# Column terms added by GpSimd instead of TensorE, row terms after the second norm, a rebuilt order, and 24 unused matmuls at the start

## The reference, cut to what matters

```
xn  = layernorm(x)                                   # x: 2 batches x 1024 tokens x 2048
q   = lambda v, s, z: (clip(round(v/s + z), 0, 255) - z) * s
x   = x + q(xn, s1, z1) @ q(ctx, s2, z2)            # ctx: 2 x 2048 x 2048
y   = layernorm(x)
x   = x + y @ W + bias + lora(y)                     # W: 2048 x 2048, LoRA rank 32 + 32 shared, 8 gates
```

## Time and profile before

| | |
|---|---|
| median of 3 runs | 1066.53 us |
| the profiled execution: its time | 1063.74 us |
| its span on the core | 1061.7 us |
| TensorE busy | 1003.1 us (94%) |
| VectorE, ScalarE, GpSimd busy | 532.3, 311.5, 163.4 us |
| mean granted TensorE clock | 0.989 of full speed |

### The profile page before, as it was taken

The page is one execution under the profiler, slowest core; times in us unless marked ns, Lnnn a source line. Parts: engine busy times, 40 slices in busy tenths (PEclk is TensorE's granted clock), DMA queues, the critical chain, the costliest instruction groups (busy, mean ns, idle before and its releaser), DMA issues.

```text
span 1061.7 us, 12294 instructions
## 1 busy us (share of the span) xinstructions
PE 1003.1 (94%) x4791; PEld 472.9 (45%) x4791; DVE 532.3 (50%) x764; ACT 311.5 (29%) x266; POOL 163.4 (15%) x199
## 2 busy tenths in 40 slices
PE   2778999799999999999999999999999999999996
PEld 1345444355544444444444444445544444444442
DVE  6754677879655455463423555987632023014010
ACT  4666731322032132232223743532121021003000
POOL 3101100101102211311510000020104004004110
PEclk9989999899999999999999999999999999999998
DMA  8869682767735446338599844456935025004010
GB/s 365 255 192 368 260 346 96 184 139 183 201 127 195 168 149 212 138 112 251 204 299 262 336 179 159 80 166 147 222 110 169 20 80 187 20 30 158 10 42 27
DMA packets 124392, 181.70 MB, mean 171 GB/s; under 512 B 96064, under 2 KB 96064, under 8 KB 111808
## 3 DMA queue, kind: packets, MB, share of 16 engines
q1 hardware_dynamic: 109600, 118.25, 37.3%
q0 software_dynamic: 13600, 58.73, 15.3%
q10 hardware_dynamic: 1152, 4.19, 1.0%
HBM read 128.72 MB, written 29.36 MB: 149 GB/s over the span
## 4 chain that ended last, share of the span: by engine, by line
PE 68%; DVE 11%; DMA 10%; issue 4%; ACT 3%; POOL 1%; SPq 1%; DVEq 0%; POOLq 0%; ACTq 0%
PE psum L1154 16%; PE psum L1156 16%; PE psum L1155 16%; PE psum L987 15%; DMA stage<-in_w 2%; DMA x<-in_x 2%; PE psum L1177 2%; DMA lhs<-in_lora_b 1%; DVE ring L1396 1%; DMA xn<-in_x 1%; DVE stats L1421 1%; DVE hl L1441 1%; DVE stats L1308 1%; DMA bias_sb<-in_bias 1%; DMA lhs<-ap_st 1%
## 5 line engine op out<-in xcount | busy, mean ns | idle before, releaser
L1154 PE MATMUL psum<-ring,lhs 128*128 128x512 f16 x1024 | 388.8, 380 | 9.4 <-DMA lhs<-hl 7.4
L1155 PE MATMUL psum<-ring,lhs 128*128 128x512 f16 x1024 | 388.8, 380 | 0.0
L1156 PE MATMUL psum<-ring,lhs 128*128 128x512 f16 x1024 | 388.8, 380 | 0.0
L987 PE MATMUL psum<-ring,lhs 128*128 128x512 bf16 x1024 | 235.2, 386 | 9.0 <-DMA lhs<-ap_st 7.1
L987 PEld LDWEIGHTS psum<-ring,lhs 128*128 128x128 bf16 x1024 | 101.4, 99 | 134.8 <-issue 15.4
L1154 PEld LDWEIGHTS psum<-ring,lhs 128*128 128x128 f16 x1024 | 100.3, 98 | 132.3 <-issue 10.1
L1156 PEld LDWEIGHTS psum<-ring,lhs 128*128 128x128 f16 x1024 | 100.4, 98 | 121.3 <-issue 0.8
L1155 PEld LDWEIGHTS psum<-ring,lhs 128*128 128x128 f16 x1024 | 100.3, 98 | 119.9 <-issue 0.8
L1448 DVE SCALAR_TENSOR_TENSOR x<-psum,sc,x 128x512 f32<-128x512 f32 (+1 forms) x64 | 45.3, 746 | 182.2 <-PE psum L1166 181.4
L748 ACT ACTIVATE ring<-stage,sc 128x2048 f16<-128x2048 f32 x32 | 63.7, 2002 | 202.6 <-PE psum L1156 159.4
L617 POOL TENSOR_TENSOR x<-x,bias_sb 128x512 f32<-128x512 f32 (+1 forms) x64 | 87.7, 1396 | 173.5 <-DVE xn L1431 98.2
(11 more groups left out here) (158 smaller groups left out, 644.9 us busy)
## 6 DMA issues: line engine op xcount, KB each, us to landing
stage<-in_w SPq DMA_DIRECT2D x38, 1024.0 KB, 6.0
stage<-in_ctx_in SPq DMA_DIRECT2D x30, 1024.0 KB, 7.9
out<-x POOLq DMA_DIRECT2D x64, 256.0 KB, 3.5
x<-in_x POOLq DMA_DIRECT2D x8, 1024.0 KB, 11.9
xn<-in_x POOLq DMA_DIRECT2D x8, 1024.0 KB, 7.3
x<-in_x POOLq DMA_DIRECT2D x4, 2048.0 KB, 15.9
lhs<-in_lora_a POOLq DMA_DIRECT2D x4, 1024.0 KB, 6.9
lhs<-in_lora_b SPq DMA_DIRECT2D x4, 1024.0 KB, 13.3
```

The costliest lines, as they stand in the source:

```text
L987: last = pe.matmul(psum[:, t, :], lhs_q[:, k, t * P:(t + 1) * P], ring_q[:, g, j % 2, u, :], start=(k == 0), stop=False)
L1154: pe.matmul(psum[:, t, :], hi, ring[:, g, 0, u, :], start=(kk == 0), stop=False)
L1155: pe.matmul(psum[:, t, :], hi, ring[:, g, 1, u, :], start=False, stop=False)
L1156: last = pe.matmul(psum[:, t, :], lo, ring[:, g, 0, u, :], start=False, stop=False)
```

## The change

1. Blocks other than block 0 of batch 0 lose the matmuls of L1021 (`column_term`, 8 a block, 7 blocks) and VectorE's `column_low`. ScalarE writes the whole column term to `bias_sb` in float32 (`col_row`), and GpSimd adds it to `x2` before the eviction (`add_column`, 8 a block); `evict1` waits for `with_col`.
2. The row term is added after `norm2` of a tile, 2048 columns at once, since a number per token does not change a layer norm; `add_bias` of block 0 waits for it.
3. Other orders: the loads, transposes and statistics of the opening, the LoRA loads and copies, VectorE's stream at the hand-over, and `base0_pair`, which starts on tile 0 alone.
4. Ahead of the first `turn`, TensorE does 24 matmuls of 512 columns into bank 0 whose result nobody reads.

The diff, cut to its core:

```
@@ sync
-            load_ctx(0, 1, [0, 1])
             for t in range(PT, TILES):
                 turn_q(t)
+            load_ctx(0, 1, [0, 1])
...
             load_lora_b(0)
+            load_lora_b(1)
             load_ctx(0, 1, [2])
-            load_lora_b(1)
-            load_ctx(0, 1, [3])
             load_lora_b(2)
             load_lora_b(3)
+            load_ctx(0, 1, [3])
+            sp.wait_ge(be_full, 8)
             load_ctx(0, 2, [0, 1])
...
-                        turn_y(b, 1)
+                        turn_high(b, 1)
+                    if g == 2 and isinstance(j, int) and j == 0:
+                        turn_low(b, 1)
@@ gpsimd
-            load_x([4, 5])
+            load_x(range(4, TILES))
             root_pair(1)
-            load_x([6, 7])
...
+            load_lora_a(0)
+            load_lora_a(1)
             root_pair(2)
-            load_lora_a(0)
             root_pair(3)
-            load_lora_a(1)
...
+            def add_column(b, j, tiles=range(TILES)):
+                pool.wait_ge(col_row, b * NBLK + j)
+                if b:
+                    pool.wait_ge(res_in[j], 16)
+                for t in tiles:
+                    if b == 0:
+                        pool.wait_ge(relued, t + 1)
+                    v = x2[:, t, j * NW:(j + 1) * NW]
+                    pool.tensor_tensor(v, v, bias_sb[:, :], ALU.add).then_inc(with_col, 1)
...
-                        pool.wait_ge(normed2, b * TILES + t + 1)
+                        pool.wait_ge(with_row, b * TILES + t + 1)
...
                     largest(1, MX_A, PW_A)
+                    add_column(b, 1, range(2))
                     largest(2, MX_B, PW_B)
-                    store_a(b)
-                    largest(3, MX_W, PW_W)
+                    add_column(b, 1, range(2, TILES))
                 else:
                     load_residual(b, NBLK - 1)
-                    store_a(b)
+                    add_column(b, 0)
+                    add_column(b, 1)
+                store_a(b, [0, 1])
+                add_column(b, 2)
+                store_a(b, [2, 3])
+                add_column(b, 3, [0])
+                if b == 0:
+                    largest(3, MX_W, PW_W)
+                add_column(b, 3, range(1, TILES))
@@ scalar, column(j)
-                    act.activation(col_parts[:, n % 2, :], psum[:, CB, :], ACT.Copy, scale=D1).then_inc(col_hi, 1)
+                    if n == 0:
+                        act.activation(col_parts, psum[:, CB, :], ACT.Copy, scale=D1).then_inc(col_hi, 1)
+                    else:
+                        if n > 1:
+                            act.wait_ge(with_col, (n - 1) * TILES)
+                        act.activation(bias_sb[:, :], psum[:, CB, :], ACT.Copy, scale=D1F).then_inc(col_row, 1)
+
+                def row_term(t):
+                    act.wait_ge(rows_ready, b + 1)
+                    act.activation(x2[:, t, :], x2[:, t, :], ACT.Identity, bias=RC[:, t:t + 1]).then_inc(with_row, 1)
@@ scalar, batch 0 after the row sums
-                    act.wait_ge(rows_ready, b + 1)
-                    for t in range(TILES):
-                        row_term(t, 0, 1)
                     for c in range(NBLK):
                         for k in range(c * KC, (c + 1) * KC):
                             a_eff_out(k)
-                        ctx_block(b, 1, [c])
+                        if c < 2:
+                            ctx_block(b, 1, [c])
+                    ctx_block(b, 1, [2])
                     for c in range(NBLK):
+                        if c == NBLK - 1:
+                            ctx_block(b, 1, [3])
                         b_eff_out(c)
-                        if c:
-                            row_term(c - 1, 1, NBLK)
@@ scalar, second norm
                     split_hi(b, t)
                     if t + 1 < TILES:
                         root(b, 1, t + 1)
+                    row_term(t)
...
                 split_hi(b, 1)
+                w_groups(b, 0, [2, 3])
                 root(b, 1, 2)
-                w_groups(b, 0, [2, 3])
+                row_term(0)
+                row_term(1)
@@ tensor
+                pe.wait_ge(ident_ready, 1)
+                pe.wait_ge(pats, 6)
+                for n in range(24):
+                    pe.matmul(psum[:, 0, :], ones_b, any_row, start=True, stop=True)
                 turn(0)
                 turn(1)
...
+                if t == CB and (b or j):
+                    pe.wait_ge(col_row, b * NBLK + j)
...
-                    for t in range(2):
-                        tile_in(t)
-                        bank_free(k, t)
-                    for g in range(NG):
+                    tile_in(0)
+                    bank_free(k, 0)
+                    pe.wait_ge(converted, grp_w(b, 0, 0) + 1)
+                    base_group(0, 0)
+                    high_in(1)
+                    bank_free(k, 1)
+                    high_group(1, 0)
+                    pe.wait_ge(converted, grp_w(b, 0, 1) + 1)
+                    base_group(0, 1)
+                    low_in(1)
+                    low_group(1, 0)
+                    base_group(1, 1)
+                    for g in range(2, NG):
@@ vector, evict1
-                dve.wait_ge(with_row, (2 + j) * TILES + t + 1 if b else min(j, 1) * TILES + t + 1)
+                if b or j:
+                    dve.wait_ge(with_col, (b * NBLK + j - 1) * TILES + t + 1)
@@ vector, opening
             stats1(4)
             round1(2)
+            round1(3)
             stats1(5, range(2))
-            round1(3)
...
+            scale_rows([4, 5], 3)
             head_group(3)
-            stats1(6)
-            scale_rows([4, 5], 3)
+            stats1(6, range(2))
+            round1(4)
+            stats1(6, range(2, NBLK))
+            round1(5)
             stats1(7)
             variance([6, 7])
-            round1(4)
             scale_rows([6, 7], 4)
-            round1(5)
@@ vector, hand-over
                 evict1(b, j, 3)
-                early_stats2(b, 2)
-                late_stats2(b, 2)
+                w_group(b, 0, 0)
                 low2(b, 1)
                 evict1(b, j, 4)
                 evict1(b, j, 5)
-                w_group(b, 0, 0)
                 w_group(b, 0, 1)
                 evict1(b, j, 6)
                 evict1(b, j, 7)
                 w_group(b, 0, 2)
+                stats2(b, 2)
                 w_group(b, 0, 3)
```

More of the change, by code:

```diff
@@ L1120, in first_by_tile @@
                         column_sum(b, j)
-                    first = 1 if tail else TILES // 2 - 1
-                    if t >= first:
-                        column_term(b, j, range(t + 1) if t == first else [t])
                 if tail:
@@ L1129, in first_by_tile @@
                             group1(j, t, g)
-                    column_term(b, j, range(TILES - tail, TILES))
             def base(b, t, j, k, gi):
@@ L1146, in last_bases, with high_group, low_group @@
                         base_group(t, g)
+            def high_group(t, g):
+                for u in range(GU):
+                    kk = g * GU + u
+                    hi = lhs[:, 0, kk, t * P:(t + 1) * P]
+                    pe.matmul(psum[:, t, :], hi, ring[:, g, 0, u, :], start=(kk == 0), stop=False)
+                    pe.matmul(psum[:, t, :], hi, ring[:, g, 1, u, :], start=False, stop=False)
+            def low_group(t, g):
+                for u in range(GU):
+                    lo = lhs[:, 1, g * GU + u, t * P:(t + 1) * P]
+                    pe.matmul(psum[:, t, :], lo, ring[:, g, 0, u, :], start=False, stop=False)
             def base_group(t, g):
```

97 lines of the change are left out of this document (49 added, 48 removed).

## The result

| | before | after |
|---|---|---|
| median | 1066.41 us (4 runs, 1064.5 to 1067.35) | 1082.03 us (4 runs, 1078.03 to 1082.87) |
| ratio, 95% interval | | 1.0141 [1.0117, 1.0165] |
| profiled execution's span | 1061.7 us | 1076.5 us |

What follows compares the result with a forecast made beforehand. TensorE, busy 1003.1 of 1061.7 us, was taken as the bound. Terms -8.6 - 4.6 - 4.8 - 4.5 - 5.2 - 2.3 + 4.5 = -25.5, +0.5 for the clock, gave -25: median about 1041 us, range 1033 to 1055.

Steps and rivals of the forecast that it cites:

- column matmuls: First product: 56 of 64 matmuls go, 12.1 us of PE time; GpSimd's 56 adds instead cost PE nothing.
- Opening and LoRA: Start of batch 0: earlier transposes give -8.6 us, LoRA B waits removed -4.6; block 1 starts at 96.2.
- row terms: ScalarE: 48 instructions become 16 of 2048 columns, each hidden while VectorE does low2; costed at nothing.
- Fewer matmuls: First product: 0.216 us saved per column matmul; -4.8 us in batch 0's blocks 1 and 2, -5.2 in batch 1.
- Hand-over: Start of second product: PE starts without pause and VectorE's chain gains; -4.5 us in batch 0, -2.3 in batch 1.
- Contention: GpSimd and VectorE on shared SBUF ports, moved add_bias meeting norm2 and hand-over meetings: +4.5 us, bounds 0 and 9.
- Rival C: GpSimd's adds pace the blocks, from 3.45 us an add; at 4.2 us the time is 1081 us; chance 0.03.
- 24 unused matmuls: Ahead of the first turn: up to 0.7 us late or 0.8 faster, hidden both ways; 0.
- -7.5 predicted for batch 1: Batch 1: -5.2 us from fewer matmuls in blocks 0 to 2 and -2.3 from VectorE's hand-over chain.

Runs made afterwards that it cites:

- e1: The changed kernel with GpSimd's first three all-reduces replaced by an elementwise operation: 1052.42 us, ratio 0.9866.
- e8: e4 with the hand-over to the second product of the kernel before, in both batches: 1051.41 us, ratio 0.9878.
- e10: The changed kernel with VectorE's context groups 2 and 3 ahead of the evictions of block 1 in batch 0: 1074.59 us, ratio 1.0071.
- e6: The kernel before with only the new order of loads, transposes and VectorE's statistics in the opening, LoRA loads included: 1062.34 us, ratio 0.9971.
- e4: The changed kernel with batch 0's column terms by matmul as before and batch 1's by GpSimd: 1051.59 us, ratio 0.9877.
- e5: e4 with the column terms of batch 1 by matmul too, so no GpSimd column adds anywhere: 1057.36 us, ratio 0.9926.
- e11: The changed kernel with all 56 adds, largest(1) and largest(2) together, largest(3) behind block 3's adds, context groups first, no unused matmuls: 1055.75 us, ratio 0.9915.
- e12: e11 with the column sum of blocks 1 and 2 behind tile 2 instead of tile 0, both batches: 1053.15 us, ratio 0.9893.
- e3: The changed kernel without the 24 unused matmuls: 1079.07 us, ratio 1.0149.
- e9: The kernel before with only the row terms moved behind norm2 of each tile: 1066.31 us, ratio 1.0006.
- e7: The kernel before with one 128x1 GpSimd add between all-reduces largest(1) and largest(2) in batch 0: 1067.01 us, ratio 0.9998.
- e2: The changed kernel with largest(1) and largest(2) together and all eight adds of block 1 behind them: 1071.73 us, ratio 1.0057.

## Why the prediction was wrong

The sign was wrong because of one step, and two terms were too large. The step is worth the 29.6 us between after and e1. The rest, 11 us from my 1041 to e1's 1052.42, is for the larger part the hand-over, 6.8 us in the sum and 0 in e8.

*The step that failed* is in "column matmuls": that `add_column(0,1)` "stands behind four stores and the first all-reduce, with `largest(2)` in its middle; the evictions behind it are needed only a block later", and that `largest(3)` and the seven last adds "come before" the evictions that need them. I counted instructions (1.27 us an add, 0.4 an all-reduce) and not what lies between two kinds of them. The trace of before had it: its first all-reduce began at 120.34, with GpSimd idle for 6.3 us before it, put down to "issue", after its last store, and its first add at 209.02 had 8.4 us of the same ahead of it. In its place the runs show 34.5 us of change-over on the chain of after, 29.6 us of time from after to e1. The second half of the sentence was wrong as well: evictions held by the adds hold the context groups behind them on VectorE (after) and bank 7 for the column sum (e10).

*Opening and LoRA* were right to a microsecond: the LoRA matrices at 67.0 (67.7), block 1 at 96.6 (96.2), the transpose wait gone. But the term alone is not worth 13 us: e6, with the orders of that term and not the others, gave 3.4. The row terms I had costed at nothing, and the order of the copies I had not costed at all; one of them, or both, let the 13 us arrive.

*Fewer matmuls* pay where nothing disturbs the adds: 5.8 of 6.9 us in batch 1 (e4 against e5). In batch 0 the term (-4.8) is there once no change-over stands among the adds: from the column sum of block 1 to that of block 3 e1 takes 55.7 us, e4 59.1 and the kernel before 60.6. In the whole time it is not seen: e1, e11 and e12 are no quicker than e4.

*Hand-over, -4.5 and -2.3:* wrong in size. In e4 the fourth group's load came late, behind a transpose, which I had left out of the step "load of W's fourth group (about 5.4 here)": it was issued 32.1 us after block 3's column sum and landed at 38.1. So `norm2(2)` gained 0.8 us (44.1 to 43.4) where I had 4.5, and the row terms took some 1.6 back. In after itself it came 45.6 us behind that column sum, 1.5 later than before. TensorE's pause at `delta0(2)`, predicted at some 4 us, was 2.83 in after and 3.18 in e4. e8 prices the whole term at 0, within some 5 us.

*Contention, +4.5:* present, but not where I had put it. Beside the moved `add_bias` three `norm2` of batch 0 took 1.48 us instead of 1.35, 0.13 each where I had 0.4. The larger part came from the column adds, which I had not counted here. In batch 1 of after one context group met a series of eight adds, as both timelines show:

```profile
603.96 9.85 POOL L618 TENSOR_TENSOR x<-x,bias_sb 128x512 f32<-128x512 f32 x8
...
609.67 4.70 DVE L1421 TENSOR_SCALAR ring<-ring 128x2048 bf16<-128x2048 int16 x1
```

The groups over the whole run, by line, count, busy time, mean and idle time, against the earlier trace rows:

```profile
L618 POOL TENSOR_TENSOR x<-x,bias_sb 128x512 f32<-128x512 f32 x56 | 83.3, 1519 | 64.2 <-ACT bias_sb L917 40.6 <-issue 23.5
...
L1421 DVE TENSOR_SCALAR ring<-ring 128x2048 bf16<-128x2048 int16 x30 | 27.9, 932 | 51.6 <-ACT ring L768 51.5
```

That context group took 4.70 us instead of 0.69 and ended 0.6 us after the last add: it was held over more than three adds, not for one. The evictions beside the same series stayed at 0.75. The Trainium skill (SBUF — State Buffer, Who interferes with whom) has both: a VectorE `tensor_scalar` in a mode that takes the shared ports is fully blocked by a GpSimd instruction that holds them, and an instruction with one SBUF input outside such a mode is not touched; that a series of adds can keep the ports from one to the next is this trace's. Over all 30 groups it is 7.2 us of VectorE (27.9 - 20.7). In e4, with adds in batch 1 alone, it is 5.7 us (26.4 - 20.7), of which the time shows 1 to 2 (6.9 less 5.8 or 5.2), less than the spread of the runs.

*Rival C* named GpSimd and 1081 us, and the time came out there, but not by its mechanism: it decided from 3.45 us an add, and the adds took 1.52. I had given it 0.03, having looked for the price of the adds and not of what stands between them. My argument that much of VectorE's 19.31 us in a block is evictions was also loose: eight of 0.746 us are 6.0.

*The 24 unused matmuls* at 0, and *row terms* at nothing, held (e3, e9).

**Left open.** The stretch of loops between the batches took 303.0 us before and 303.6 to 307.3 in the other kernels; TensorE's pauses there sum to 3.1 us before, 5.7 in after and 7.2 in e12. Batch 1 took 471.0 us before, 469.7 in after, and from 465.6 (e3) to 475.5 (e10) in kernels whose batch 1 is the same as that of after. These are single profiles, and no experiment addressed the differences. So the -7.5 predicted for batch 1 is neither shown nor refuted by the two profiles; what is shown is e4 against e5.

## What to carry to other kernels

GpSimd's stream is priced by its changes of kind, not only by its instructions: look for idle time put down to "issue" ahead of an all-reduce or behind one, and keep elementwise work that someone waits for away from it, or let the all-reduces stand together. When an instruction is made later, find every reader of the bank or buffer that it frees, the odd one first: here the column sum uses bank 7 one tile after the block's start. And a reordering that "costs nothing" may be what another part's gain rests on; the opening alone was worth 3.4 us, though block 1 started 12 us earlier.

## What the runs showed of the hardware

- GpSimd's change-over: 5.6 to 5.8 us from adds to an all-reduce and 6.9 to 9.5 from there to adds in after; around the 0.47 us add of e7 it was the other way round, 10.39 to the all-reduce and 6.75 from it. Two all-reduces together take one change-over (10.05 us to the adds in e2, 10.52 in e11). From stores to an all-reduce GpSimd stood 6.33 us before and 8.30 in after. Why it varies is not shown.
- A context group on VectorE (2048 columns, int16 to bf16) took 4.70 us instead of 0.69 beside a run of eight GpSimd adds, where one meeting in the earlier trace rows had cost 0.80.
- 24 matmuls in idle time, from 5.5 to 12.9 us, made the first needed matmuls at 15.1 quicker (1.05 us for 16 instead of 1.87) and changed nothing in the time that can be measured: 1079.07 without, 1082.03 with.
